# Sums over four key tiles, made by GpSimd and VectorE, as the source of the softmax denominators

## The reference

```
scores = jnp.einsum('bhsd,bhtd->bhst', q, k) * scale
attn = jax.nn.softmax(scores, axis=-1)
o = jnp.einsum('bhst,bhtd->bhsd', attn, v_c)
```

## Time and profile before

| | |
|---|---|
| median of 3 runs | 842.99 us |
| the profiled execution | 842.36 us, span 840.5 us |
| TensorE matmul busy over the span | 92% |
| VectorE, ScalarE, GpSimd busy | 73%, 60%, 49% |
| units 0 to 7 of the first attention start at | 59.39, 93.90, 128.94, 163.94, 199.47, 234.96, 270.63, 305.64 us |

### The profile page before, as it was taken

One profiled execution on the slowest core, in us unless ns is written; L12 is line 12 of the kernel. 1 busy time (PEld: TensorE's weight loads), 2 busy tenths in 40 slices (PEclk: granted clock), 3 DMA queues, 4 the chain that ended last, 5 costly groups with the idle time before them and its releaser, 6 DMA issues.

```text
span 840.5 us, 13859 instructions
## 1 busy us (share of the span) xinstructions
PE 770.1 (92%) x4602; PEld 451.0 (54%) x4602; DVE 613.3 (73%) x1611; ACT 505.5 (60%) x864; POOL 408.9 (49%) x466
## 2 busy tenths in 40 slices
PE   5899999999999998989999988699999999999986
PEld 2454444444444433579888864355555555554554
DVE  6877687786877798865237668687778777787555
ACT  3335665757656576346546445467777777776772
POOL 3506866667757583707060686967344132220121
PEclk9879999999999999999999999999999999999999
DMA  9400000000000000123131020000000000000001
...
DMA packets 14539, 25.35 MB, mean 30 GB/s; under 512 B 3174, under 2 KB 9192, under 8 KB 14344
## 3 DMA queue, kind: packets, MB, share of 16 engines
...
...
## 4 chain that ended last, share of the span: by engine, by line
PE 36%; DVE 14%; POOL 6%; issue 4%; ACT 2%; DMA 0%; ACTq 0%; POOLq 0%; DVEq 0%
PE ps L1677 6%; PE ps L1762 6%; PE ps L1742 4%; DVE ps L2534 3%; PE ps L1648 3%; DVE mx_part L2537 3%; PE ps L1630 2%; PE ps L1640 2%; PE ps L1631 2%; PE ps L1632 2%; POOL xnT L659 1%; PE ps L1595 1%; PE ps L1770 1%; PE ps L1831 1%; PE ps L1543 1%
## 5 line engine op out<-in xcount | busy, mean ns | idle before, releaser
L2053 DVE TENSOR_REDUCE mx_part<-ps 128x1 f32<-128x512 f32 x256 | 163.8, 682 | 59.1 <-PE ps L1322 58.3
L1114 ACT ACTIVATE pt<-ps 128x1024 f32<-128x1024 f32 (+1 forms) x160 | 149.7, 938 | 69.5 <-PE ps L1742 68.0
L907 ACT ACTIVATE pt<-ps 128x512 f32<-128x512 f32 x256 | 140.9, 596 | 70.4 <-PE ps L1347 64.0
L1677 PE MATMUL ps<-rounded 128*128 128x128 f32 (+2 forms) x352 | 123.6, 384 | 12.1 <-DVE mx_part L2534 4.5
L2534 DVE CUSTOM_DVE_ANT_0 ps<-ps,wm 128x128 f32<-128x128 f32 (+3 forms) x256 | 119.6, 518 | 18.8 <-PE ps L1677 17.7
L859 ACT ACTIVATE rounded<-ps 128x512 fp32r<-128x512 f32 (+3 forms) x160 | 94.3, 591 | 63.8 <-PE ps L1311 22.3
L1347 PE MATMUL ps<-rounded 100*128 100x512 f32 x256 | 120.8, 484 | 10.6 <-ACT pt L907 9.7
L722 POOL TENSOR_SCALAR_AFFINE_SELECT pt<-pt 128x512 f32<-128x512 f32 x64 | 39.9, 636 | 167.7 <-ACT pt L1114 167.6
L1742 PE MATMUL ps<-rounded 128*128 128x512 f32 (+2 forms) x352 | 115.5, 368 | 0.7 <-ACT rounded L859 0.7
L1322 PE MATMUL ps<-rounded 98*128 98x512 f32 x256 | 105.7, 431 | 2.2 <-DVE mx_part L2053 1.2
L2537 DVE TENSOR_REDUCE mx_part<-ps 128x1 f32<-128x512 f32 x128 | 82.4, 686 | 31.0 <-PE ps L1677 30.8
...
...
## 6 DMA issues: line engine op xcount, KB each, us to landing
...
```

Source lines behind the costliest of these rows:

```text
L907: nc.scalar.activation(pt0(k, i), ps[:, ST0_BANKS[i % 2], :], ACT.Exp, scale=SCALE0).then_inc(exp_done, 1)
L1114: nc.scalar.activation(pt[:, 4 * (t % 2) + 2 * g:4 * (t % 2) + 2 * g + 2, 0:w], ps[:, ST1_BANKS[2 * g]:ST1_BANKS[2 * g] + 2, 0:w], ACT.Exp ...
L1677: ins = mm(bank[:, o:o + w], queries1(u, i), keys[:, 0:w], start=(o == 0), stop=(o == parts[-1][1]))
L2053: v.tensor_reduce(mx_part[u % 2][:, o:o + 1], ps[:, max_bank(u, n), :], AX_X, ALU.max).then_inc(max_done, 1)
```

## The change

In units 0 to 6 the two pair sums of four key tiles are added once more, in place, to a quad sum: pieces 0 and 1 by GpSimd (`quad_adds` of the GpSimd block), pieces 2 and 3 by VectorE (`quad_adds` of the VectorE block). TensorE multiplies two quad sums a unit with the ones instead of four pair sums: the first at key tile 6, the second at key tile 2 of the next unit. The pair adds now wait for quad sums of both engines where the set of tiles that they overwrite was an operand of one. Reciprocals move later, past the new group. Unit 7 stays with pairs.

```diff
-DEN0_AT, DEN0_LAST_AT = {3: 0, 5: 1, 7: 2}, {4: 0, 5: 1, 7: 2}
+DEN0_AT, DEN0_LAST_AT = {6: 0}, {4: 0, 5: 1, 7: 2}
...
         def sums(u, j):
-            return pair_sum[j % 2 + (2 if u >= SUMS_MOVE else 0)]
+            k = (0, 1, 1, 0)[j] if u + 1 < U0 else j % 2
+            return pair_sum[k + (2 if u >= SUMS_MOVE else 0)]
...
                     pool.wait_ge(exp_done, (u * TS + 2 * j + 1) * HQ + i + 1)
-                    if i == 0 and G >= 2:
-                        pool.wait_ge(den_mm, G - 1)
+                    if i == 0 and (u or j > 1):
+                        if j % 2:
+                            pool.wait_ge(den_mm, u * NQSUM + (1 if j == 3 else 0))
+                        else:
+                            pool.wait_ge(quad_pool, HP * (u * NQSUM + j // 2))
+                            pool.wait_ge(quad_dve, HP * (u * NQSUM + j // 2))
...
+            def quad_adds(u, q):
+                pool.wait_ge(pair_add, (u * NPAIR + 2 * q + 2) * HQ)
+                for i in range(HP):
+                    a, b = (sums(u, 2 * q + k)[i] for k in range(2))
+                    nc.gpsimd.tensor_tensor(a, a, b, ALU.add).then_inc(quad_pool, 1)
...
                     if u and j == 1:
                         contexts_out(u - 1)
+                    if j % 2 and u + 1 < U0:
+                        quad_adds(u, j // 2)
                     if j == 1 and u + 1 < U0:
                         low_max(u + 1)
...
-                    if k == 1 and u:
-                        denominators(u - 1, 1 - pp, NPAIR - 1)
+                    if k == 2 and u:
+                        denominators(u - 1, 1 - pp, NQSUM - 1)
...
+            def quad_adds(u, q):
+                dve.wait_ge(pair_add, (u * NPAIR + 2 * q + 2) * HQ)
+                for i in range(HP, HQ):
+                    a, b = (sums(u, 2 * q + k)[i] for k in range(2))
+                    v.tensor_tensor(a, a, b, ALU.add).then_inc(quad_dve, 1)
...
                 pieces(0, 2, 3, 4)
-                pieces(1, 0, 1, 2, 3, 4)
+                pieces(1, 0, 1, 2)
+                if u:
+                    quad_adds(u - 1, 1)
+                pieces(1, 3, 4)
+                z_lo_at(1)
+                pieces(2, 0, 1, 2)
                 rden(0)
-                z_lo_at(1)
+                pieces(2, 3, 4)
                 rden(1)
-                pieces(2, 0)
-                rden(2)
-                pieces(2, 1, 2, 3, 4)
-                rden(3)
                 if (u, 2) in OUT_AT:
                     add_output1(OUT_AT[u, 2])
-                pieces(3, 0, 1, 2, 3, 4)
+                pieces(3, 0)
+                rden(2)
+                pieces(3, 1, 2)
+                rden(3)
+                pieces(3, 3, 4)
                 z_lo_at(3)
                 pieces(4, 0, 1, 2, 3, 4)
                 if u + 1 < U0:
                     split_max(u + 1)
                 z_lo_at(4)
+                if u + 1 < U0:
+                    quad_adds(u, 0)
```

26 lines of the change are left out of this document (19 added, 7 removed).

## The result

The kernel after the change takes 869.96 us (median of 4 runs, 867.82 to 872.99) against 842.19 us (839.82 to 844.04, 4 runs): ratio 1.032, 95% interval 1.030 to 1.035. It is slower, as forecast, by 27.8 us and not by 9. The profiled execution has a span of 871.2 us; before it was 840.5.

What follows compares the result with a forecast made beforehand. TensorE was taken as the bound; unit changes -1.9 + 4.2 + 3.2 + 1.5 + 1.1 + 0.9 = +9.0 us on 842.36 gave 851.4, as median 852.0 us. Range 840 to 860, the forecast's own 848 to 856.

Steps and rivals of the forecast that it cites:

- the two waits: Wait A, for pair 0 behind VectorE's adds, and Wait B, at key tile 5, both delaying TensorE.
- Wait A: Pair 0 waits for VectorE's adds, starts 3.6 us later; exponentials stretch, scores matmul (3,1) goes 2.0 us late.
- the forecast for these five: Units 1 and 2 +2.1 us each, units 3 and 4 +1.6 each, unit 5 +1.5.
- Unit 7 ... 0 to +3, I take +0.9: VectorE arrives about 1 us late in unit 7, first adds for unit 6 beside GpSimd's L593; +0.9 us.
- Wait B: At key tile 5 both engines add at once; TensorE's last maxima matmul waits 2.0 us, 1.0 without blocking.
- its 118.75: Time in us, on unit 1's clock, when VectorE reaches its new adds at key tile 5; before, free at 117.49.
- What is removed: Two of four groups of ones matmuls in 7 units: 14 x 0.97 = 13.6 us off TensorE.
- Unit 0: First unit, without wait at pair 0, reciprocals or contexts; adds delay tile 5 by 0.8; taken as -1.9 us.
- unit 6: Only the groups gain; `turn_max` waits about 1.5 us for `low_max`; 0 to +2, taken as +1.1 us.
- VectorE becomes the bound: Rival: VectorE's delay reaches back to key tile 4, 0.6 to 1 us more a unit; 857 to 862; chance 0.15.
- a wait for one instruction: Key tile 5: VectorE's first add waits for GpSimd's last, then adds take 0.55 and 0.65; TensorE waits 2.0 us.
- one for each add in turn: Key tile 5, other end: each VectorE add is blocked by GpSimd in turn, 1.3 us more.

Runs made afterwards that it cites:

- group_twice: Kernel before, with the first group of ones matmuls of units 0 to 6 issued twice; ratio 1.006.
- pair0_at_9: Kernel before, with GpSimd's first sum of units 1 to 5 held until VectorE's maximum that ends 9.34 us into the unit; ratio 1.020.
- filled_gaps: Changed kernel, with TensorE repeating maxima matmuls in the gaps of key tiles 2 and 3 in units 1 to 5; ratio 1.026.
- unit6_pairs: Changed kernel, with quad sums in units 0 to 5 only, unit 6 keeping pair sums and four groups; ratio 1.019.
- late_weights: Changed kernel, with GpSimd's four early expert weight subtractions in unit 7 moved behind the contexts; ratio 1.026.
- spare_adds: Kernel before, with VectorE making the change's number of adds at the same places in units 0 to 5, on tiles nobody reads; ratio 1.033.
- adds_spread: Changed kernel with third tile set, unit 6 of pair sums, VectorE's key tile 1 adds one maximum earlier, first four-tile sum later; ratio 1.030.

## Why the prediction was wrong, point by point

- **The direction, the bound and the two waits: right.** TensorE is the bound (group_twice). Wait A came at its place: pair 0 at 100.52 in a unit that begins at 91.17, 9.35 us in, where the forecast (103.0 in a unit at 93.90) had 9.1, and the exponentials 1.21 to 1.23 apart instead of 1.26.
- **The term that failed is what "Wait A" made of three waits on TensorE: their price was counted as time waited, and nothing was put down for the clock behind them.** The earlier trace rows showed 1.00, and the whole sum was made in instruction times at that level. pair0_at_9 shows the missing term with nothing else changed. In units 1 to 5 the changed kernel is 20.4 us longer. At 37.4 us a unit, the length at full clock in filled_gaps, unit6_pairs and late_weights, it would be 10.3; the forecast for these five was 8.9. The other 10.2 us are what these units took beyond that, all at a clock below 1.00: about a third of the loss. (For unit 5, which none of these runs has at full clock, 37.4 is assumed.)
- **"Unit 7 ... 0 to +3, I take +0.9": mis-sized, 11.1.** The mechanism was named (VectorE arrives late and first adds for unit 6, beside GpSimd's subtractions) but not followed to VectorE's own four sums: 8.23 us instead of 2.5, exponentials behind each of them, then half clock. unit6_pairs takes all 11 back; late_weights shows that at least 3.5 of them are the clash.
- **Wait B: the mechanism right, the size too large in unit 1.** 1.15 us and not 2.0, with VectorE's adds at 1.70 us. VectorE came at 117.31 in a unit that began 2.7 us earlier, so 1.3 us later on the unit's clock than I had it, and by then GpSimd was at the end of its adds (its last one ended at 117.83). The terms of the forecast add up to 118.5 and not to its 118.75 (117.49 - 0.97 + 1.28 + 0.72), a slip of 0.2 that decides nothing. In units at full clock with the same instructions the wait was 1.48 us (unit 2 of unit6_pairs).
- **What is removed: 0.97 a group, measured 0.85** (group_twice, at the margin). Over 14 groups 1.7 us too much. Unit 0 gained 1.3 instead of 1.9; unit 6 lost 2.2 instead of 1.1, with `turn_max` waiting for `low_max` as forecast, but 2.23 us and not 1.5, and the clock at 0.95.
- Together: 10.2 of clock, 1.4 of waits in units 1 to 5, 10.2 of unit 7, 1.1 of unit 6 and 0.6 of unit 0 are the 23.5 us between +9.0 and +32.5.
- **The rival "VectorE becomes the bound"** (857 to 862) was nearest, and is not the cause either: in spare_adds VectorE is busy 31 of 40 us. What costs there is not its total but two-input adds that take 3.23 us and not 1.29 while GpSimd adds.
- **The rule that was cited** from the Trainium skill (SBUF — State Buffer, "SBUF: two separate sides", an exclusive lock for the whole instruction) holds: two adds take 1.29 us with GpSimd idle, and 1.70, 3.23 and 7.77 beside it. In adds_spread the one add waited not through one instruction of GpSimd but through six, so neither a wait for one instruction nor one for each add in turn, the two cases of the forecast, is the upper end.
- The Trainium skill's page TensorE: Matmul & The Clock Gate, section "Part 1: The HAM clock gate (the "warmup" mystery)", says that the clock follows how busy TensorE has lately been. The trace agrees (0.50 from 108 to 110 us, behind waits of 0.71, 0.73 and 0.48 us). It would have been the rival that was missing.

**What stays open.** The same waits do not always bring the clock down: in unit6_pairs unit 2 has 0.71, 0.72 and 0.49 us as unit 1 has, but 1.00 and 37.4 us against 0.84 and 42.1. No run here tells what decides it, so the clock's part can be measured over several units and not forecast for one. And the 11 us of unit 7 were not divided between the clash, the late start and the clock. What the later reciprocals cost was not run by itself.
